# Spare wide passes on TensorE in the last head pair, the routing and the last logits; key and query chunks moved inside a pair

## The chip, the cores and the metric

## The reference

One layer over 1250 nodes of 1024 features, in three parts: a graph convolution over 20,000 edges, a kernelized attention with 16 heads of 64 and 256 random features, and a mixture of 8 experts of which each node takes two.

```python
xn = _layernorm(x)
x = x + gnn(xn, edge_index, W, b) + mix(xn[None], Wq, bq, ..., orf)[0]
x = x + ffn(_layernorm(x)[None], gate_w, gate_b, expert_w, expert_b)[0]
...
# mix: phi(y) = (exp(y @ orf.T / dk**0.25 - |y|^2 / (2 sqrt(dk))) + 1e-6) / sqrt(m)
kv = jnp.einsum('bhlm,bhld->bhmd', k_phi, v)
num = jnp.einsum('bhlm,bhmd->bhld', q_phi, kv)
out = num / einsum('bhlm,bhm->bhl', q_phi, k_phi.sum(2))[..., None]
...
# ffn: logits of 8 experts, the two largest kept, softmax over them, weighted sum of their outputs
```

## The kernel before

Products that need full precision are made of three single-pass products of a high and a low part (`xh`, `xl`; `hw[:, wi, 0]`, `hw[:, wi, 1]`). Nodes lie in 10 tiles of 128 (the last has 98 rows). The engines run side by side and are ordered by semaphores; each engine takes its instructions in the order in which the code gives them, and a wait holds all that stands behind it on that engine.

The stages are the graph's counts and products (to about 370 us), the attention (to about 964 us), the output projection in two passes of ten row tiles (to about 1093 us), the gate's logits and the routing (to about 1130 us), and the experts.

**The attention** handles two heads at a time, so there are 8 pairs. Seven run in a loop and the eighth is written out with `last=True`; its branches differ because no next pair's projections stand between its steps. In a pair TensorE runs:

- `project_third(j, wi, i, between)` (L1806 to L1808): a third of the nodes through the key, value or query weights of one pair, 24 passes of 416 or 418 columns into bank i. Behind each k but the last it can call `between(k)`, which puts another step there.
- `key_features(j, h, i)` (L1821, L1822): the random features of two tiles' keys of head h, four passes into bank 3 or 4 by turns. It waits until ScalarE has taken the exponential of the chunk two before it (`exp_done`).
- `turn_values` (L1832): values transposed into banks 6 and 7; VectorE copies them to `vt` (L1376).
- `key_values(h, ...)` (L1844): features times values into bank 5. It waits for all five key chunks of the head with their epsilon added (`kph_ready`) and for the last copied values (`aux_evac`).
- `query_features(h, i)` (L1856, L1857): two passes into bank 3 or 4 by turns; it too waits for the exponential (ScalarE, L1055) of the chunk two before it. VectorE adds the epsilon (L1363, `qph_ready`).
- `outputs(h, i)` (L1867): five tiles' attention outputs of a head; the exponentials of head 1's queries wait for both `outputs(0, ...)`, since the features of both heads share `qphi`.
- `turn(i)` (L1876): the outputs transposed; VectorE copies them to `attnT` (L1398).

In the last pair ScalarE and VectorE also make the high and low slabs of the output projection's weights (`high_slab`, `low_slab`, L1048 and L1368) between these steps. VectorE ends with two slabs, the low part of the first row tile (L1459), two copies of turned outputs and a last small low part (L1477), for which `row_tile` (L1791 to L1793) waits. GpSimd makes the weight slabs of the second pass (`split_weights`) and then the constants of the routing.

**The logits** of a tile (L1949) are eight products of 128x128 activations with 8 columns of gate weights, two passes each. `turn_x2(t)` (L1959) transposes the normalized tile before. VectorE's `choose(t)` (L1497) takes the two largest. Behind the last tile VectorE makes `both`, TensorE multiplies it (L1978, L1979: `route_done`), VectorE makes positions and one-hots (`slot_hot`), TensorE the slots (L1987) and, after three more one-hot products, the gates (L1996), between which the first gathered tile is transposed (L2008). Then the experts begin (L2022 to L2025).

Of the kernel before, what the change touches and what calls it, by code (L numbers as in the profile page):

```python
# [8 lines left out]
P = 128  # L9
N, D = 1250, 1024  # L10
TT = -(-N // P)
# [50 lines left out]
def gps_layer(nc, x, dst_pairs, src_cols, dst_cols, wg, bg, wq, bq, wk, bk, wv, bv, wo, bo, orf,  # L62
# [6 lines left out]
    with ctx:  # L69
# [217 lines left out]
        def bank(b, n=CW):  # L287
            return PB[:, 512 * b:512 * b + n]
# [356 lines left out]
        def _(pool):  # L645
# [114 lines left out]
            def split_weights(r, c):  # L760

                for k in range(KT):
                    split_slab(r, c, k)
# [23 lines left out]
            with pool.Fori(0, KT - 1) as j:  # L787
# [6 lines left out]

            attention_over(pool)
            split_weights(ro, 1)
            g.iota(iota8[:, :, :], [[0, TT], [1, E]], base=0, channel_multiplier=0,
                   allow_small_or_imprecise_dtypes=True).then_inc(s_route_const, 1)
            g.iota(thr[:, :, :], [[0, E], [P, TT]], base=P, channel_multiplier=0,
# [871 lines left out]
        def _(pe):  # L1671
# [141 lines left out]
            def key_features(j, h, i):  # L1813
# [8 lines left out]
                    ins = mm(o, nk[:, h, at], orfn[:, h], start=False, stop=True)  # L1822
                ins.then_inc(phi_done, 1)

            def pair(j, last):

                def turn_values(i):
                    t0, nt = VALUE_TILES[i]
                    pe.wait_ge(aux_evac, 12 * j + i + 1)
                    pe.wait_ge(vt_ready, 3 * j + (1, 2, 3, 3)[i])  # L1830
                    for q in range(nt):
                        ins = nc.tensor.transpose(bank(6 + i % 2)[:, q * P:(q + 1) * P],  # L1832
                                                  vT[:, (t0 + q) * P:(t0 + q + 1) * P], ident[:, :])
                    ins.then_inc(aux_done, 1)

                def key_values(h, first, last_one):

                    pe.wait_ge(kv_evac, START + 2 * j + h)
                    pe.wait_ge(kph_ready, 10 * j + 5 * h + 5)
                    pe.wait_ge(aux_evac, 2 + 12 * j + 4)  # L1840
                    for i in range(first, last_one):
                        m, t = i // TT, i % TT
                        n = LAST if t == TT - 1 else P
                        ins = mm(bank(5)[:, m * (DK + 1):(m + 1) * (DK + 1)], kphi[0:n, t, m * P:(m + 1) * P],  # L1844
                                 vt[0:n, t, h, :], start=(t == 0), stop=(t == TT - 1))
                    if last_one == MH * TT:
                        ins.then_inc(kv_done, 1)
# [23 lines left out]
                def turn(i):  # L1871

                    t0, nt = VALUE_TILES[i]
                    pe.wait_ge(aux_evac, 12 * j + 8 + i + 1)
                    for q in range(nt):
                        ins = nc.tensor.transpose(bank(6 + i % 2)[:, q * P:(q + 1) * P], att[:, t0 + q, :], ident[:, :])  # L1876
                    ins.then_inc(aux_done, 1)
# [8 lines left out]
                turn_values(2)  # L1886
                key_features(j, 1, 0)
                turn_values(3)
                key_values(0, 0, MH * TT)
                key_features(j, 1, 1)  # L1890
                project_third(j, 2, 0)
                key_features(j, 1, 2)
                key_features(j, 1, 3)
# [6 lines left out]
                query_features(0, 1)  # L1900
                if last:
                    for i in range(2, 6):
                        query_features(0, i)
                    query_features(1, 0)
                else:
                    project_third(j + 1, 0, 0, lambda k: query_features(0, 2 + k // 4) if k % 4 == 2 else None)
                    project_third(j + 1, 0, 1, lambda k: query_features(0, 4 + k // 4) if k % 4 == 2 else None)
                    query_features(1, 0)
# [3 lines left out]
                outputs(0, 1)  # L1912
                if last:
                    for i in range(2, 5):
                        query_features(1, i)
                else:
                    project_third(j + 1, 0, 2, lambda k: query_features(1, 2 + k // 2) if k % 2 == 1 else None)
                query_features(1, 5)
                pe.wait_ge(kv_evac, START + 2 * j + 2)
                outputs(1, 0)  # L1920
                outputs(1, 1)
                if not last:
                    project_third(j + 1, 1, 0)
                turn(0)
                turn(1)
                if not last:
                    key_features(j + 1, 0, 0)
                    project_third(j + 1, 1, 1)
                turn(2)
                turn(3)  # L1930

            for i in range(3):
                project_third(0, 0, i)
# [6 lines left out]
                for p in range(2):  # L1940
                    row_tile(ro, 0, 2 * g + p, p)

            def logits(t):
                if t >= 2:
                    pe.wait_ge(lg_taken, t - 1)
                for k in range(KT):
                    if k % 4 == 0:
                        pe.wait_ge(x2t_evac, 2 * t + k // 4 + 1)
                    ins = mm(bank(4 + t % 2, E), x2T[:, t % 2, k, :], gw[:, k, :], start=(k == 0), stop=(k == KT - 1))  # L1949
                ins.then_inc(lg_done, 1)  # L1950

            def turn_x2(t):
# [15 lines left out]
                    logits(t - 3)  # L1968
            logits(TT - 3)
            turn_x2(TT - 2)  # L1970
            logits(TT - 2)
            turn_x2(TT - 1)
            logits(TT - 1)

            pe.wait_ge(s_both, 1)
            whole, rest = slice(0, TT - 1), TT - 1
            for b, left in ((0, upper), (1, ones)):
                mm(bank(b, (TT - 1) * E), left[:, :], both[:, whole, :].rearrange("p t e -> p (t e)"), start=True, stop=True)  # L1978
                ins = mm(bank(b)[:, rest * E:TT * E], left[0:LAST, :], both[0:LAST, rest, :], start=True, stop=True)  # L1979
            ins.then_inc(route_done, 1)  # L1980

            for i in range(2 * TT):
                if i % TT == 0:
# [45 lines left out]
            def expert(e, par, last):  # L2030
                more, begin = tiles(pe, e)
                with pe.Fori(0, more + 1) as i:
                    tile(begin + i, e, par)

            gates(0)
            pe.wait_ge(s_cnti, 1)
            for h in range(2):
# [59 lines left out]
```

## Time and profile before

| what | value |
|---|---|
| median of 3 runs | 1418.61 us (1415.19 to 1418.94) |
| profiled execution, its own time | 1417.75 us |
| its span | 1416.2 us |
| mean granted clock of TensorE | 0.973 |
| busy: TensorE / VectorE / ScalarE / GpSimd | 96% / 56% / 40% / 26% |
| chain that ended last: TensorE / VectorE / ScalarE | 85% / 5% / 3% |

A matmul's duration in a row runs to its modelled end, and the passes overlap; how far the starts lie apart tells what one costs in a stream. A merged row (x20) runs from the first start to the last end. "Idle before" is counted from the modelled end of the instruction before.

### The profile page before, as it was taken

To read this page: it belongs to the slowest core of one execution; us is meant where nothing else is said; L and a number is where in the kernel's file an instruction comes from. 1 tells how busy PE (TensorE), PEld (TensorE's weight loads), DVE (VectorE), ACT (ScalarE), POOL (GpSimd) and SP (SyncE) were. 2 spreads that over 40 slices of the span, in tenths; PEclk is the share of its full clock that TensorE was granted. 3 is DMA by queue.
4 is the path that set the end of the run, shared out by engine and by line. 5 is a ranking of instruction groups with operands and counts; after the bars stand their busy time and mean duration, and the time that the engine had idled before them with its cause. 6 is when DMAs were issued, how large, how long until landed. Compare 5 with 4: busy or idle time off the path is not lost.

```text
span 1416.2 us, 25340 instructions
## 1 busy us (share of the span) xinstructions
PE 1354.4 (96%) x8233; PEld 1197.6 (85%) x8234; DVE 789.3 (56%) x1680; ACT 572.3 (40%) x953; POOL 364.1 (26%) x375
## 2 busy tenths in 40 slices
PE   6999999999999999999999999999999599999996
PEld 3567778999999999999999999987888588888885
DVE  7867464454466565656565656564454734444641
ACT  8543332211355454545454545451122234444440
POOL 4323333254210101010101010005023133333432
PEclk9999999999999999999999999978999599999998
DMA  5112112455200000000000000013244567777853
GB/s 185 51 49 68 42 64 68 134 158 150 64 31 16 30 15 30 15 30 15 30 15 30 15 30 0 1 60 98 72 166 148 208 183 218 220 213 211 287 134 58
DMA packets 58102, 127.78 MB, mean 90 GB/s; under 512 B 7627, under 2 KB 28827, under 8 KB 58049
## 3 DMA queue, kind: packets, MB, share of 16 engines
q1 hardware_dynamic: 48016, 96.79, 20.6%
q0 software_dynamic: 10032, 30.30, 8.7%
q8 instruction: 31, 0.51, 0.1%
q14 instruction: 23, 0.18, 0.0%
HBM read 91.46 MB, written 37.43 MB: 91 GB/s over the span
## 4 chain that ended last, share of the span: by engine, by line
PE 85%; DVE 5%; ACT 3%; issue 3%; DMA 1%; DVEq 0%; POOL 0%; POOLq 0%; SPq 0%; ACTq 0%
PE PB L1701 8%; PE PB L1806 7%; PE PB L1808 7%; PE PB L1807 7%; PE PB L2022 6%; PE PB L2023 6%; PE PB L2025 6%; PE PB L1844 5%; PE PB L1867 4%; PE PB L1751 3%; PE PB L1791 3%; PE PB L1752 3%; PE PB L1753 3%; PE PB L1792 3%; PE PB L1793 2%
## 5 line engine op out<-in xcount | busy, mean ns | idle before, releaser
L1806 PE MATMUL PB<-xh,hw 128*128 128x416 f32 (+1 forms) x576 | 203.8, 354 | 0.0
L1808 PE MATMUL PB<-xh,hw 128*128 128x416 f32 (+1 forms) x576 | 202.9, 352 | 0.0
L1807 PE MATMUL PB<-xl,hw 128*128 128x416 f32 (+1 forms) x576 | 202.8, 352 | 0.0
L2022 PE MATMUL PB<-mwh,mth 128*128 128x512 f32 x368 | 147.8, 402 | 0.3 <-issue 0.3
L2023 PE MATMUL PB<-mwl,mth 128*128 128x512 f32 x368 | 143.9, 391 | 0.0
L719 POOL CAST hw<-hraw 128x1024 fp32r<-128x1024 f32 x24 | 25.2, 1048 | 418.4 <-DVE qphi L1363 197.3
L1701 PE MATMUL PB<-ohs,ohd 128*128 128x512 bf16 x564 | 114.1, 349 | 0.3 <-DVE ohs L1226 0.3
L2025 PE MATMUL PB<-mwh,mtl 128*128 128x512 f32 x368 | 113.7, 390 | 0.0
L1807 PEld LDWEIGHTS PB<-xl,hw 128*128 128x128 f32 x576 | 108.6, 189 | 1.2
L1806 PEld LDWEIGHTS PB<-xh,hw 128*128 128x128 f32 x576 | 108.6, 189 | 1.2
L1808 PEld LDWEIGHTS PB<-xh,hw 128*128 128x128 f32 x576 | 108.5, 188 | 1.0
L1623 DVE TENSOR_TENSOR mtl<-PB,mth 128x512 fp32r<-128x512 f32 x46 | 31.8, 691 | 132.4 <-ACT mth L1141 132.4
L1226 DVE TENSOR_SCALAR ohs<-iota,sc 128x1280 bf16<-128x1280 f16 x188 | 102.8, 547 | 0.0
L1701 PEld LDWEIGHTS PB<-ohs,ohd 128*128 128x128 bf16 x564 | 45.7, 98 | 66.0 <-DVE ohs L1226 34.4
L1779 PE MATMUL PB<-hh,AT 128*128 128x256 f32 x400 | 98.2, 287 | 2.7 <-DVE hr L1252 2.7
L1780 PE MATMUL PB<-hr,AT 128*128 128x256 f32 x400 | 97.4, 285 | 0.0
L1751 PE MATMUL PB<-wqh,xh 128*128 128x256 f32 x320 | 92.1, 288 | 0.0
L1752 PE MATMUL PB<-wql,xh 128*128 128x256 f32 x320 | 90.5, 283 | 0.0
L1753 PE MATMUL PB<-wqh,xl 128*128 128x256 f32 x320 | 90.4, 283 | 0.0
L1225 DVE TENSOR_SCALAR ohd<-iota,dc 128x128 bf16<-128x128 f16 x188 | 59.8, 318 | 51.8 <-PE PB L1701 45.2
L1055 ACT ACTIVATE qphi<-PB 128x416 f32<-128x416 f32 (+1 forms) x96 | 48.3, 514 | 95.0 <-PE PB L1857 87.4
L1035 ACT ACTIVATE kphi<-PB 128x512 f32<-128x512 f32 x80 | 46.2, 598 | 96.2 <-PE PB L1844 50.6
(304 smaller groups left out, 3103.7 us busy)
## 6 DMA issues: line engine op xcount, KB each, us to landing
mraw<-expert_w SPq DMA_DIRECT2D x64, 512.0 KB, 5.8
count_rests<-ATf POOLq DMA_DIRECT2D x9, 640.0 KB, 3.3
xrow<-x SPq DMA_DIRECT2D x40, 128.0 KB, 3.0
y_scratch<-xrow SPq DMA_DIRECT2D x40, 128.0 KB, 1.9
yrow<-y_scratch SPq DMA_DIRECT2D x20, 256.0 KB, 2.9
x2n_half<-xhat SPq DMA_DIRECT2D x20, 256.0 KB, 2.4
out<-x SPq DMA_DIRECT2D x9, 512.0 KB
ATf<-wg SPq DMA_DIRECT2D x32, 128.0 KB, 2.8
```

The costliest lines, as they stand in the source:

```text
L1226: v.tensor_scalar(ohs[:, p, :], iota[:, :], sc[:, ds(col, 1)], None, ALU.is_equal).then_inc(oh_ready, 1)
L1701: ins = mm(PB[:, 1536 * s + c0:1536 * s + c0 + n], ohd[:, p, :], ohs[:, p, c0:c0 + n], start=False, stop=False, skip_group_check=True)
L1751: mm(o, xh[:, k, at], wqh[q % 2][:, k, :], start=(k == 0), stop=False)
L1752: mm(o, xh[:, k, at], wql[q % 2][:, k, :], start=False, stop=False)
L1753: ins = mm(o, xl[:, k, at], wqh[q % 2][:, k, :], start=False, stop=(k == KT - 1))
L1779: mm(o, AT[:, b, at], hh[:, q % 2, b, :], start=(b == 0), stop=False)
L1806: mm(bank(i, n), hw[:, wi, 0, k, :], xh[:, k, c0:c0 + n], start=(k == 0), stop=False)
L1807: mm(bank(i, n), hw[:, wi, 0, k, :], xl[:, k, c0:c0 + n], start=False, stop=False)
L1808: ins = mm(bank(i, n), hw[:, wi, 1, k, :], xh[:, k, c0:c0 + n], start=False, stop=(k == KT - 1))
L2022: mm(y[c], mth[:, k, :], mwh[par][:, k, c * CW:(c + 1) * CW], start=(k == 0), stop=False)
L2023: mm(y[c], mth[:, k, :], mwl[par][:, k, c * CW:(c + 1) * CW], start=False, stop=False)
L2025: ins = mm(y[c], mtl[:, k, :], mwh[par][:, k, c * CW:(c + 1) * CW], start=False, stop=(k == KT - 1))
```

## The change

It adds two helpers for TensorE. `spare(n)` issues n passes of 512 columns into bank 0 from operands that lie there, `meanwhile(n)` the same into bank 6 from the first slab of the first expert's weights. Nothing reads what they write before it is overwritten. 32 spares stand in the last pair and none in the others. Ten `meanwhile` passes stand ahead of and inside the last two tiles' logits, four behind them, 20 behind the routing product and 12 before the gates. In every pair `key_features(j, 1, 1)` stands ahead of `key_values(0, ...)`. In the seven pairs of the loop, the head 1 query chunks 2, 3 and 4 stand behind k = 2, 4 and 6 of the next pair's third projection, where they stood behind k = 1, 3 and 5. GpSimd waits for the first row tile before it writes the routing constants.

```diff
             attention_over(pool)
             split_weights(ro, 1)
+            pool.wait_ge(ro.done, 1)
             g.iota(iota8[:, :, :], [[0, TT], [1, E]], base=0, channel_multiplier=0,
...
+            def spare(n):
+
+                for _ in range(n):
+                    mm(bank(0), orfh[:, 0:P], xh[:, 0, 0:CW], start=True, stop=True)
+
             def pair(j, last):
...
                 turn_values(3)
+                key_features(j, 1, 1)
                 key_values(0, 0, MH * TT)
-                key_features(j, 1, 1)
                 project_third(j, 2, 0)
...
                 if last:
                     for i in range(2, 6):
+                        spare((0, 0, 0, 2, 5, 2)[i])
                         query_features(0, i)
                     query_features(1, 0)
...
                 outputs(0, 1)
                 if last:
                     for i in range(2, 5):
+                        spare(2)
                         query_features(1, i)
+                    spare(1)
                 else:
-                    project_third(j + 1, 0, 2, lambda k: query_features(1, 2 + k // 2) if k % 2 == 1 else None)
+                    project_third(j + 1, 0, 2, lambda k: query_features(1, 1 + k // 2) if k in (2, 4, 6) else None)
                 query_features(1, 5)
                 pe.wait_ge(kv_evac, START + 2 * j + 2)
                 outputs(1, 0)
                 outputs(1, 1)
                 if not last:
                     project_third(j + 1, 1, 0)
+                if last:
+                    spare(3)
                 turn(0)
+                if last:
+                    spare(1)
                 turn(1)
                 if not last:
                     key_features(j + 1, 0, 0)
                     project_third(j + 1, 1, 1)
+                if last:
+                    spare(2)
                 turn(2)
+                if last:
+                    spare(1)
                 turn(3)
+                if last:
+                    spare(9)
...
-            def logits(t):
+            def meanwhile(n):
+
+                for _ in range(n):
+                    mm(bank(6), mwh0[:, 0, 0:P], mwh0[:, 0, 0:CW], start=True, stop=True)
+
+            def logits(t, between=0):
...
                     ins = mm(bank(4 + t % 2, E), x2T[:, t % 2, k, :], gw[:, k, :], start=(k == 0), stop=(k == KT - 1))
+                    if between and k % 2 == 0:
+                        meanwhile(between)
                 ins.then_inc(lg_done, 1)
...
             turn_x2(TT - 2)
-            logits(TT - 2)
+            pe.wait_ge(mw_high, 1)
+            meanwhile(2)
+            logits(TT - 2, 1)
             turn_x2(TT - 1)
-            logits(TT - 1)
-
+            logits(TT - 1, 1)
+
+            meanwhile(4)
             pe.wait_ge(s_both, 1)
...
             ins.then_inc(route_done, 1)
-
+            meanwhile(20)
...
+            meanwhile(12)
             gates(0)
```

## Rows read from the trace of the kernel before

**Rows 1.** the page's slices of the span: busy tenths of TensorE, and its granted clock
```profile
PE   6999999999999999999999999999999599999996
...
PEclk9999999999999999999999999978999599999998
```

**Rows 2.** windows: us; PE, PEld, DVE, ACT, POOL busy (instructions); PEclk; DMA share; GB/s
```profile
935.00:937.50 2.50, 2.20 (x10) 1.82 (x9) 1.73 (x6) 2.06 (x5) 0.00 (x0) 0.69 0.02 7
...
970.00:972.50 2.50, 2.50 (x12) 2.08 (x11) 0.00 (x0) 0.00 (x0) 2.34 (x4) 0.99 0.39 139
```

**Rows 3.** timeline, PE, last pair: start, us, line, operation, count [idle before <- releaser]
```profile
934.71 0.42 PE L1856 MATMUL PB<-tk,orfh 128*128 128x416 f32 x1 [1.10 <-DVE nk L1347]
...
935.99 0.71 PE L1856 MATMUL PB<-tk,orfh 128*128 128x418 f32 x1 [0.30 <-ACT qphi L1055]
...
936.85 4.37 PE L1867 MATMUL PB<-kvs,qphi 128*128 128x65 f32 x20
...
964.68 0.79 PE L1791 MATMUL PB<-wh,sth 128*128 128x512 f32 x1 [2.92 <-DVE stl L1477]
```

**Rows 4.** windows, as in rows 2, at the routing
```profile
1099.00:1100.50 1.50, 1.16 (x8) 1.15 (x8) 0.05 (x1) 0.72 (x2) 0.00 (x0) 0.76 1.20 369
...
1130.50:1132.00 1.50, 1.50 (x7) 1.25 (x8) 1.43 (x5) 0.00 (x0) 0.71 (x3) 1.00 1.03 415
```

**Rows 5.** timeline, PE, the gate's logits
```profile
1094.27 3.85 PE L1949 MATMUL PB<-gw,x2T 128*128 128x8 f32 x32
...
1099.38 3.19 PE L1949 MATMUL PB<-gw,x2T 128*128 128x8 f32 x16 [0.34 <-ACT x2T L1116]
...
1104.30 3.55 PE L1949 MATMUL PB<-gw,x2T 128*128 128x8 f32 x16
```

**Rows 6.** waits of PE, 467.5 to 903.3 us: total, times, longest
```profile
PE PB L1844 <- DVE vt L1376: 3.3, 6, 0.6
PE PB L1856 <- ACT qphi L1055: 2.9, 6, 0.5
```

**Rows 7.** timeline, PE, the seventh pair
```profile
834.32 4.68 PE L1844 MATMUL PB<-vt,kphi 128*128 128x65 f32 x40 [0.56 <-DVE vt L1376]
838.81 0.36 PE L1821 MATMUL PB<-orfh,tk 128*128 128x256 f32 x1
...
839.36 0.35 PE L1806 MATMUL PB<-xh,hw 128*128 128x418 f32 x1
...
877.41 0.46 PE L1856 MATMUL PB<-tk,orfh 128*128 128x416 f32 x1 [0.49 <-ACT qphi L1055]
```

**Rows 8.** timeline, ACT, the seventh pair
```profile
832.37 0.60 ACT L1035 ACTIVATE kphi<-PB 128x512 f32<-128x512 f32 x1 [0.23 <-PE PB L1822]
...
876.87 0.89 ACT L1055 ACTIVATE qphi<-PB 128x418 f32<-128x418 f32 x2
```

**Rows 9.** timeline, DVE, the seventh pair
```profile
880.99 0.38 DVE L1363 TENSOR_SCALAR qphi<-qphi 128x416 f32<-128x416 f32 x1
```

**Rows 10.** timeline, PE, passes of the output projection at two clocks
```profile
969.96 0.45 PE L1791 MATMUL PB<-wh,sth 128*128 128x512 f32 x1
...
1082.05 0.39 PE L1792 MATMUL PB<-wl,sth 128*128 128x512 f32 x1
1082.28 0.39 PE L1793 MATMUL PB<-wh,stl 128*128 128x512 f32 x1
```

**Rows 11.** timeline, DVE, end of the last pair
```profile
960.93 1.28 DVE L1368 TENSOR_TENSOR wl<-raw,wh 128x512 fp32r<-128x512 f32 x2
```

**Rows 12.** timeline, PE, the routing and the first expert pass
```profile
1119.37 0.76 PE L1987 MATMUL PB<-hott,hotr 128*128 128x70 bf16 x10 [7.51 <-DVE hotr L1586]
...
1126.43 1.06 PE L1996 MATMUL PB<-hotg,hotr 128*128 128x105 bf16 x10 [4.88 <-DVE hotg L1618]
...
1130.39 0.53 PE L2022 MATMUL PB<-mwh,mth 128*128 128x512 f32 x1 [0.29 <-issue]
```

**Rows 13.** timeline, DVE, the last tile's choice
```profile
1107.89 0.17 DVE L1497 TENSOR_TENSOR lg<-PB,gb 128x8 f32<-128x8 f32 x1 [0.65 <-PE PB L1949]
```

## The prediction, made before the change was run

> **What bounds the kernel now.** I read the page's slices first. TensorE (PE) is busy nine tenths or more in nearly every slice, and PEclk dips twice: in the 27th and 28th slice (the last pair of heads) and in the 32nd (the routing) [rows 1]. So the time is TensorE's, and it can fall in two ways: less idle PE time in the long pair loop, or a higher granted clock in the dips. The windows show these from near. In the first the clock leaves its high level (2.4 GHz) at about 935.9 us, is at its low one (1.2 GHz) for 34 us, and is high again from 970 [rows 2]. Just before the fall PE was idle for 1.10 and 0.30 us [rows 3]. In the second it falls in the window that begins at 1099.0, and the one from 1130.5 is high again [rows 4]. Ahead of that fall lies no long idle time but a run of the gate's passes over 8 columns, 32 in 3.7 us [rows 5].
>
> Then the waits of one pair. In the six pairs from 467 to 903 us PE waited in the key products (L1844) 3.3 us in all for the copy of the values, and in the query features (L1856) 2.9 us for an exponential [rows 6]: 0.56 and 0.49 us a pair [rows 7].
>
> **The change part by part.** *Key chunk moved (8 pairs).* key_features(1, 1) goes ahead of key_values(0). Its four passes take 0.55 us where they stand, from 838.81 to 839.36 [rows 7]. In the new place PE is free from about 833.6 (the wait of 0.56 us is counted from the modelled end of the pass before) until 834.32, when the copied values are there [rows 7]. The bank it writes needs the exponential that ends at 832.97 [rows 8]: it is there. So the passes fit into the wait, and the third projection starts right behind the key products. A switch from narrow to wide passes costs about 0.08 us more: 0.47 us a pair gained. ScalarE's next exponential waits for the key products, which start as before; nothing comes later.
>
> *Query chunks moved (7 pairs).* The three query chunks inside the projection stand one step of k later, so three more passes of 0.19 us lie ahead of the one that waits until 877.41 for the exponential begun at 876.87 [rows 7, 8]. The wait shrinks to under 0.1 us, and one step fewer remains behind it: 0.56 us gained. What could be late next is outputs(1, 0), which wants VectorE's fourth eps pass; this ends at 881.37 [rows 9], and PE would arrive at about 881.9. Bounds of either move: nothing, if the neighbour engine only moves the wait, and 0.56. I take 7 x 1.03 + 0.47 = **7.7 us**.
>
> *Spares in the last pair.* 32 passes of 128x512, each into a bank that nobody reads. No row shows such a pass itself; the nearest are the output projection's, of the same width: 0.23 us apart at the high level [rows 10], and at the low one twelve between 964.68 and 969.96, 0.44 [rows 3, 10]. Nine stand in the idle time before the old fall: 2.1 us of work for 1.4 us of waits [rows 3] and 0.3 of a third; the last two delay one query chunk by 0.46, which the 0.30 us wait behind it nearly pays. With no hole left there I expect the clock to stay high. The chain is then, from 936.0: a query chunk 0.46; outputs(0, 0), 20 passes, which took 4.37 us at the low level [rows 3] and should take 2.2, as 40 of the same form take 4.49 in the key products [rows 7]; another chunk and outputs(0, 1), to 941.3. Here the next exponential starts only after outputs(0, 1), so PE waits until 942.1 with two spares inside; four query chunks and five spares to 944.8; outputs(1, 0) and (1, 1) to 949.2; three spares 0.7; the turns, paced by VectorE's copies, to 951.7. Now VectorE is last: from its two slabs (960.93 now) to the first pass of the output projection (964.68) lie 3.75 us [rows 3, 11], none of them TensorE's. So the projection begins at about 955.5 instead of 964.68: **9.1 us**, rounded down. The last nine spares (2.1 us) lie beside these 3.75; without this cover they would cost 2.1. The first passes of the projection, twelve at 0.44, take 0.23 each: **2.5 us**. Bounds of the two terms: all of 11.6, or the fourth rival.
>
> *The wait on GpSimd* stands behind split_weights, which keeps GpSimd busy from 970 on [rows 2], with sixteen steps of which four fit into 2.5 us; the first row tile is done long before its end. Behind it are queued the routing constants, wanted at 1109. Zero on both sides.
>
> *Spares in the logits and the routing.* The last two tiles' logits get four each, two stand ahead, four behind; 20 come after the first routing product, 12 before the gates. But the 3.7 us run of 8-column passes gets none, and it is what stands ahead of the old fall [rows 4, 5]. I take it that the clock falls there again. Then the spares cost 0.43: the two ahead 0.85 less 0.34 that PE waited anyway, and four in each tile's logits 1.7 (3.4 to 5.1, nearest row 3.55) [rows 5]; together **+3.9 us** before the last logits are out, and VectorE's routing chain begins with them. The four behind lie in the wait for `both`. The 20 fill the 7.51 us wait for the one-hots [rows 12]: as a dense stream at the low level they resemble 964.68 to 970, where the clock came back after 5.3 us. 5.3 at 0.43 are 12 passes, the other 8 take 1.8, sum 7.1: just covered (8.6 and 1.1 too long if it stays low). Then the gates and the first transposes find the high level. From 1126.43 to 1130.39 they took 3.96 us [rows 12]; half of PE's part goes, ScalarE's and VectorE's steps stay: **-1.2 us**.
>
> A rule speaks on this last part. The trace: the clock was high from 1130.5 on, right behind 20 gate passes and 8 transposes [rows 4, 12]. The Trainium skill ("TensorE: Matmul & The Clock Gate", Part 4: PE-mode transpose) says that the full clock doesn't engage for transposes, which don't count as work in the same way. By that rule this rise should have come later; the trace disagrees.
>
> **Sum**, against the profiled execution's 1417.75 us (span 1416.2): 1417.75 - 7.7 - 9.1 - 2.5 + 3.9 - 1.2 = **1401.2 us**. That execution is 0.9 us under the median of the three runs; the forecast stays at 1401.
>
> **The rivals.** (1) *The clock holds through the logits.* The spares ahead of and inside the last two catch it in time. Then I estimate the last logits start by ScalarE's slab at 1104.1 instead of 1104.30 and run 2.6 us instead of 3.55, and VectorE, busy with three slabs until about 1107.0, makes its last choice 0.9 us earlier than at 1107.89 [rows 5, 13]; the routing products halve, 0.9; the gates gain between 0 and 1.2 (PE idles for 3 us behind its 20 spares), say 0.8. 1417.75 - 19.3 - 2.6 = 1395.9. For it: logits with a spare behind every second product are much denser. Against: the bare run is untouched. Chance 0.30; the forecast 0.46.
> (2) *The clock falls late in the last pair*, among the turns or in the last VectorE chain, where PE still idles some 1.5 us behind its nine spares. Then the projection begins slow for 5.3 us as now, 2.5 us come back, and a turn or two are slower: 1401.2 + 2.5 to 3.5, about 1404. The skill's rule on transposes (same page and section) would favour this. Against: seven spares stand among the turns and nine behind. Chance 0.12.
> (3) *The moves in the pair do nothing*: the waits come back at the next chunk, ScalarE and VectorE setting the pace. 1401.2 + 7.7 = 1408.9. Against: what the moved chunks need is there in time [rows 8, 9]. Chance 0.08.
> (4) *Slower: the spares pay at the low clock.* If it still falls at 936, 25 spares at 0.43, 10.7 us, stand on PE's path against about 4.2 us of waits (0.30 and 2.92 among them [rows 3]), +6.5; the logits +3.9, and 0.2 from 20 slow spares: 1417.75 - 7.7 + 6.5 + 3.9 + 0.2 = 1420.7. It decides from where the nine early spares don't keep the clock up. Against: the hole they fill is the only one there. Chance 0.04.
>
> **How the numbers follow.** About 0.3% (4.3 us) is what a measurement of this kernel can tell from no change. The forecast and rivals (1) to (3) lie more than that below 1418.6; (4) lies within it, or beyond with some further loss. Faster 0.94, same 0.04, slower 0.02. The range goes from 1393.5, the first rival with the upper bounds of its terms, to 1408, short of (3).
>
> **What would show it.** The waits of L1844 and L1856 in a pair are under 0.2 us, and the pairs follow each other about 1.0 us closer. The granted clock is 1.00 from 900 to the second dip, and the output projection starts 9 us closer to the last pair's key products. In the logits, spares 0.43 us apart and 5.1 us a tile (forecast), or 0.22 and 2.6 (first rival). The clock is high at the gates. The prediction is wrong if the clock drops in the last pair all the same, or holds where I let it fall.

## The result and the profile after

| | before | changed |
|---|---|---|
| median, 8 executions each | 1418.3 us (1412.2 to 1424.6) | 1402.8 us (1397.2 to 1414.1) |
| profiled execution, its own time | 1417.75 us | 1404.21 us |
| its span / mean granted clock | 1416.2 us / 0.973 | 1402.7 us / 0.988 |

The ratio changed to before is 0.9905, 95% interval 0.9879 to 0.9930: faster by about 1%. A second measurement (e9 below) gave 0.9929 (0.9908 to 0.9951).

The page's slices of the changed kernel (busy tenths of TensorE and its granted clock), which answer to [rows 1]:

```profile
PE   6999999999999999999999999999999899999996
...
PEclk9999999999999999999999999999999799999998
```

The dip at the last pair is gone, the one at the routing is shallower (7 for 5). Windows of the changed kernel, from the last pair on (columns as in rows 2):

```profile
901.70:930.00 28.30, 28.30 (x184) 27.41 (x185) 16.63 (x37) 16.48 (x31) 0.00 (x0) 1.00 0.12 38
930.00:949.60 19.60, 18.57 (x128) 16.50 (x126) 13.61 (x32) 9.61 (x19) 0.00 (x0) 1.00 0.17 55
949.60:970.00 20.40, 20.34 (x90) 16.82 (x91) 9.94 (x11) 3.75 (x4) 14.61 (x14) 1.00 0.57 168
```

and at the logits and the routing:

```profile
1076.00:1081.00 5.00, 4.96 (x46) 4.87 (x45) 4.30 (x15) 1.09 (x2) 1.27 (x2) 1.00 0.34 107
1081.00:1094.50 13.50, 13.50 (x55) 12.24 (x54) 4.72 (x11) 8.28 (x10) 0.00 (x0) 0.50 1.00 365
1094.50:1101.40 6.90, 6.67 (x20) 5.18 (x21) 4.74 (x25) 0.21 (x1) 0.00 (x0) 0.50 0.08 30
1101.40:1108.30 6.90, 4.49 (x37) 3.42 (x36) 6.56 (x17) 0.00 (x0) 0.00 (x0) 0.99 0.00 0
1108.30:1111.70 3.40, 3.40 (x10) 2.62 (x9) 3.06 (x14) 0.00 (x0) 1.81 (x2) 0.50 0.07 18
1111.70:1118.00 6.30, 3.83 (x35) 2.88 (x34) 4.01 (x8) 1.19 (x2) 2.59 (x5) 1.00 0.56 173
```

PEclk is 1.00 through the whole last pair. It falls at the logits all the same, comes back inside the 20 spares (from 1101.4), falls once more from 1108.3 to 1111.7 and is high at the gates.

In the pairs, the waits of PE from 467.5 to 901 us, against [rows 6]:

```profile
PE PB L1838 <- DVE vt L1377: 1.6, 6, 0.3
```

The key products (L1850 now) and the query features (L1862 now) are gone from the list; only the value transposes' 0.27 us is left. The end of the last pair, TensorE's timeline, against [rows 3]:

```profile
927.93 1.33 PE L1829 MATMUL PB<-xh,orfh 128*128 128x512 f32 x5
929.09 0.39 PE L1862 MATMUL PB<-tk,orfh 128*128 128x416 f32 x1
...
930.84 2.34 PE L1873 MATMUL PB<-kvs,qphi 128*128 128x65 f32 x20
...
946.31 2.35 PE L1829 MATMUL PB<-xh,orfh 128*128 128x512 f32 x9
949.66 0.50 PE L1792 MATMUL PB<-wh,sth 128*128 128x512 f32 x1 [1.00 <-DVE stl L1478]
```

The five spares (L1829) stand where PE waited 1.10 us, and the chunk behind them follows without a wait. An `outputs` of 20 passes takes 2.34 us instead of 4.37. The nine last spares end 1.00 us ahead of the output projection (2.92 us of waiting before).

For the whole document it helps to cut a trace into stages by the start of a fixed instruction. These distances come from the traces' rows, one profiled execution each:

| stage, us | before | changed | forecast of the difference | measured |
|---|---|---|---|---|
| seven pairs, first to eighth key products (L1844) | 507.97 | 501.17 | -7.2 | -6.8 |
| eighth key products to first output projection | 57.88 | 48.00 | -9.6 | -9.9 |
| output projection to the bare logits (tile 6) | 129.59 | 127.09 | -2.5 | -2.5 |
| bare logits to the last logits pass | 13.22 | 17.57 | +3.9 | +4.35 |
| last logits pass to the slots' first pass (L1987) | 11.88 | 11.89 | 0 | 0.0 |
| slots' first pass to the gates (L1996) | 7.05 | 7.05 | 0 | 0.0 |
| gates to the first expert pass (L2022) | 3.97 | 3.99 | -1.2 | 0.0 |
| first expert pass to the end | 285.8 | 285.4 | 0 | -0.4 |

The changed kernel's profiled execution reaches the first key products 1.7 us late (400.50 for 398.83). Up to there the programs differ only by one key chunk that stands in a wait, and its second trace (e9) reaches them at 399.01, so this is not the change's. With the gates' 1.2 that didn't come and the 0.45 more at the logits it makes up the 3 us by which the execution lies over the forecast of 1401.2.

### The profile page after: what moved, and what is told of

Read it like the earlier page. It is cut to its first block, busy times and chain, and to the rows that moved or that the text cites. A ratio compares the mean times of both kernels' runs of the same rounds, so it can differ in the third digit from the quotient of the medians.

```text
span 1402.7 us, 25462 instructions
## 1 busy us (share of the span) xinstructions
PE 1359.7 (97%) x8277; PEld 1203.1 (86%) x8312; DVE 789.8 (56%) x1680; ACT 571.5 (41%) x953; POOL 362.0 (26%) x375
## 4 chain that ended last, share of the span: by engine, by line
PE 88%; DVE 5%; issue 2%; ACT 2%; DMA 2%; DVEq 0%; POOL 0%; POOLq 0%; SPq 0%; ACTq 0%
PE PB L1702 8%; PE PB L1807 7%; PE PB L1809 7%; PE PB L1808 7%; PE PB L2051 6%; PE PB L2052 6%; PE PB L2054 6%; PE PB L1850 5%; PE PB L1873 5%; PE PB L1752 3%; PE PB L1792 3%; PE PB L1794 3%; PE PB L1753 3%; PE PB L1754 3%; PE PB L1793 3%
## 5 line engine op out<-in xcount | busy, mean ns | idle before, releaser
L1702 PE MATMUL PB<-ohs,ohd 128*128 128x512 bf16 (+1 forms) x530 | 110.3, 348 | 3.4 <-DVE ohs L1227 0.7
L1142 ACT ACTIVATE mth<-PB 128x512 fp32r<-128x512 f32 x46 | 27.5, 598 | 139.1 <-PE PB L2037 139.1
```

The source lines that it names most:

```text
L1702: ins = mm(PB[:, 1536 * s + c0:1536 * s + c0 + n], ohd[:, p, :], ohs[:, p, c0:c0 + n], start=False, stop=False, skip_group_check=True)
```

## The experiments

**How executions of one kernel differ.** The executions of before spread over 22 us (48 of them, 1407.8 to 1430.4). Each comes with its span and mean granted clock, so the time that it spent at the low level is 2 x (1 - clock) x span: 51 us in the fastest, 100 to 103 in the slowest two. I fitted one straight line through 130 executions of ten kernels, with one slope for all and a level for each. The slope is 0.39 us of time for a microsecond at the low clock (95% interval 0.36 to 0.42), and what is left over has a standard deviation of 1.7 us. Without the slowest execution of before neither the slope nor any level moves by more than 0.1. The level tells what an edit costs or gains at equal clock, and the mean low-clock time what it does to the clock:

| kernel | executions | mean us | low clock, mean us | level against before |
|---|---|---|---|---|
| before | 48 | 1417.7 | 69 | 0 |
| changed (with e9) | 14 | 1404.0 | 35 | -0.2 +- 1.5 |
| e1: moves only | 7 | 1406.5 | 61 | -7.9 +- 1.4 |
| e2: last pair's spares only | 12 | 1412.9 | 53 | +1.7 +- 1.2 |
| e3: logits' and routing's spares only | 12 | 1417.0 | 50 | +6.9 +- 1.3 |
| e5: moves and last pair's spares | 6 | 1402.4 | 47 | -6.7 +- 1.6 |
| e4 and e10: changed without 14 logit spares | 11 | 1401.2 | 35 | -3.3 +- 1.6 |
| e11: e4 without the last nine | 6 | 1402.0 | 36 | -2.8 +- 1.8 |
| e6: spares in two more logits | 6 | 1404.4 | 33 | +0.7 +- 1.9 |
| e7: changed without the early nine | 8 | 1407.2 | 45 | -1.0 +- 1.5 |

The slope is a mean over stages, and the +- are 95% intervals. Low-clock time in a stage where TensorE waits anyway costs less than 0.39 (e5 below shows such a stage), and an edit that removes only such time shows a level that is too high; this matters for e3, and in part for every kernel with spares at the routing.

**e1, the moves alone.**

```diff
-                key_values(0, 0, MH * TT)
                 key_features(j, 1, 1)
+                key_values(0, 0, MH * TT)
...
-                    project_third(j + 1, 0, 2, lambda k: query_features(1, 2 + k // 2) if k % 2 == 1 else None)
+                    project_third(j + 1, 0, 2, lambda k: query_features(1, 1 + k // 2) if k in (2, 4, 6) else None)
```

> The kernel before with the key and query chunks moved and no spare pass. My theory: the moves alone are worth 7.7 us by the rows; a pair's period falls from about 72.6 to about 71.6 us, whatever the clock does elsewhere, so the ratio to before is about 0.9945 (7.7 of 1418). Rival (the waits only move to the next chunk): period unchanged, ratio 1.000. A second rival: the moves thin out other stretches so that the clock falls in the loop in some executions; then single executions come out above before's slowest and the mean granted clock is lower than before's.

Measured: median 1405.1, ratio 0.9908 (0.9875 to 0.9940), more than the 0.9945 expected. The chain of its profile puts the key products every 71.6 us (470.58, 542.22, 613.85; in before 471.29, 543.74):

```profile
470.58 4.68 PE PB L1844 x40
...
542.22 4.68 PE PB L1844 x40
...
613.85 4.68 PE PB L1844 x40
```

At equal clock the level is -7.9, the forecast's 7.7. The rest of the mean's 11.2 us goes with 9 us less at the low clock, but the seven executions lie between 48 and 79 us of it and before's between 51 and 103; whether the fuller loop keeps the clock up better, or seven executions fell well, stays open. The rival "the waits only move on" is out. The second rival (clock falls in the loop) didn't show: the slowest of the seven took 1412.2 us, and the trace's loop ran at the high level.

**e8 and e12, each move alone**, the halves of e1's diff.

> The kernel before with the key chunk moved alone. By the forecast's terms the distance of one pair's key products from the next's falls by 0.47 us, from 72.6 to 72.1, and no L1844 waits over 0.2 us; the wait of the query chunk (0.49 us) stays. Rival (the wait only moves on): distance 72.6, a new wait in front of the third projection or of the next key chunk.

> The kernel before with the query chunks moved alone. By the forecast's term the distance between the pairs' key products falls by 0.56 us, from 72.6 to 72.05, and the wait of L1856 for the exponential is under 0.1 us. Measured with the key move alone: 0.43 us, and both together 0.95 to 1.0; so 0.50 to 0.56 is left for this one. Rival (the exponential is what sets the pace, and the wait only moves to the next query chunk): distance unchanged.

Measured, as distances between key products, in one execution each (1415.6 and 1412.8 us as a whole). Key move: from the second pair (470.79) to the seventh (831.71) five distances of 72.2 us, before 72.6: 0.4 us. Query move: 474.50 to 906.42, six distances of 71.99: 0.6 us. The waits of PE in the pairs, key move first:

```profile
PE PB L1856 <- ACT qphi L1055: 2.9, 6, 0.5
PE PB L1832 <- DVE vt L1376: 1.6, 6, 0.3
```

```profile
PE PB L1844 <- DVE vt L1376: 3.3, 6, 0.6
PE PB L1832 <- DVE vt L1376: 1.6, 6, 0.3
```

Each move takes away its own wait and leaves the other's as it was in [rows 6]. The two are of the size foreseen (0.47 and 0.56), and together they make what e1 has (0.95 us a pair).

The trace of e12 shows one thing more. It has no spare, and PE waits 0.96 us and 0.29 us in the last pair where before it waited 1.10 and 0.30. Its clock fell there too, at 934.4, but for 3.4 us and not for 34, and once more for 6.8 us from 954.9. Three rows of its chain:

```profile
906.42 4.65 PE PB L1844 x40
...
934.28 0.57 PE PB L1856
...
955.74 0.80 PE PB L1791
```

From the key products to the output projection it took 49.3 us, 8.6 less than before's 57.9, and 0.8 more than the 48.5 with 32 spares (e2 below). So the long dip that the spares remove is not there in every execution.

**e2, the last pair's spares alone.** The 32 `spare` passes and GpSimd's wait; no moves, nothing in the logits or behind.

> The kernel before with only the 32 spares of the last pair (and GpSimd's wait). My theory: the clock stays at its high level from the last pair to the logits in every execution, and the output projection starts 9.1 us closer to the last pair's key products than in the profile of before (964.68 - 906.79 = 57.9 us there, so about 48.8 here), and the first row tile gains 2.5 us more: 11.6 us, ratio 0.992. Rival (the clock falls late in the turns): about 8 to 9 us, with PEclk 0.50 behind the turns. Rival (in most executions of before the clock holds in the last pair anyway and the profiled one was an unlucky one): the two kernels' times overlap, and the ratio is over 0.996.

Measured: median 1414.4, ratio 0.9957 (0.9930 to 0.9984). In its profile the eighth key products to the output projection is 48.49 us (9.4 less than before's) and on to the bare logits 127.10 (2.5 less): in that execution all of the 11.9 us is there. In the mean it is 4.8 us, because the mean execution of before is not the profiled one: it has 69 us at the low clock, the profiled one 76, and 33 of the 48 have 71 or less. So the second rival (the profiled one was an unlucky one) is partly right: the times overlap, though the ratio is just under 0.996. The stages bear out the mechanism where the dip is there, and the forecast took one execution's dip for every one's.

**e3, the routing's spares alone.** Ten ahead of and inside the last logits, 4, 20 and 12 behind; no moves, none in the last pair.

> The kernel before with only the spares of the logits and the routing (10 ahead of and inside the logits, 4, 20 and 12). My theory, as the profile of the changed kernel showed it: where the clock falls in the bare logits before them, the spares cost 0.43 each and the last logits come 3.9 us later; the gates gain nothing, since the gather's landing follows: about +4 us, ratio 1.003. Where the clock holds, about -2.6 us, ratio 0.998. Rival (the spares hold the clock in most executions): ratio under 0.999.

Measured: ratio 0.9988 (0.9960 to 1.0017), no difference. In its profiled execution the clock held through the bare run of 32 narrow passes and the first of the two tiles with spares, and fell at 1112.5, inside the second, behind a wait of 2.00 us:

```profile
1100.29 3.85 PE L1959 MATMUL PB<-gw,x2T 128*128 128x8 f32 x32
...
1111.17 0.36 PE L1959 MATMUL PB<-gw,x2T 128*128 128x8 f32 x2 [2.00 <-ACT x2T L1116]
```

Bare logits to the last pass took 14.58 us, where the changed kernel has 17.57 and before 13.22. So with the clock up TensorE waits for ScalarE, and the stage is still no shorter than with a low clock and no spares. Its mean low-clock time is 20 us under before's, worth 7.6 us by the slope, and its mean is 0.7 us better. So the 20 us that were won seem to have lain mostly where TensorE waits, and its level of +6.9 can't be read as a price of passes. The fall in the bare logits, as in the changed kernel's trace, would take away only some 7 us; so the rival, that the spares hold the clock in most executions, may well be right, but one trace and a ratio with 1 in its interval don't decide it.

**e4 and e10, without the 14 logit spares.**

```diff
-            pe.wait_ge(mw_high, 1)
-            meanwhile(2)
-            logits(TT - 2, 1)
+            logits(TT - 2)
             turn_x2(TT - 1)
-            logits(TT - 1, 1)
-            meanwhile(4)
+            logits(TT - 1)
+            pe.wait_ge(mw_high, 1)
```

> The changed kernel without the spares ahead of, inside and directly behind the last two tiles' logits (14 passes); the 20 and the 12 of the routing stay. My theory: these 14 are what costs; the last logits come 3.9 us earlier than in the changed kernel's profile, the clock still rises in the 20. So about 4 us faster than the changed kernel: ratio to before about 0.988 where the changed kernel has 0.9905. Rival (without them the 20 do not lift the clock, or the logits' spares pay in the executions where the clock holds): no faster than the changed kernel, ratio 0.9905 or more.

> The changed kernel without the 14 logit spares, a second time. My theory: the 14 cost 2 to 4 us, so it is again 2 to 4 us faster than the changed kernel on this chip (about 1400 to 1401), with the same time at the low clock within 5 us. Rival (the first measurement's 2 us were chance, and the 14 are free): within 1 us of the changed kernel.

Measured: 0.9872 (0.9841 to 0.9904), and the second time 0.9893 (0.9878 to 0.9908), beside 0.9929 for the changed kernel on the same chip. The stage from the bare logits to the last pass is 14.56 and 13.90 us, 3.0 and 3.7 less than the changed kernel's 17.57 and 17.61. Low-clock time is the same, 35 us. This is the fastest kernel of the study, 2.8 us under the changed one in the mean of 11 and 14 executions; the intervals of the ratios overlap or touch, but the stage that was edited shows the difference in both pairs of traces. How much it is depends on where in the logits the clock falls: without logit spares the stage took 13.1 to 15.2 us over nine traces, with them 17.0 to 17.6 in the three traces in which the clock fell in the bare run.

**e5, no spare behind the last pair.** e4 without the 20 and the 12 too.

> The changed kernel without any spare in the logits and the routing (48 passes left out); moves and the last pair's spares stay. A line through the executions of each kernel (time against time at the low clock, which follows from the mean granted clock and the span) has so far given two prices: moves 8.2 us less at equal clock, last pair's spares 1.2 more, routing's spares 6.3 more, and 0.38 us for each us at the low clock. My theory (the parts add up): 8.2 + 5.8 = 14 us under before in the mean, about 1404.7, ratio 0.990; that is, the 48 routing spares give back nothing in sum. Rival (the 20 spares behind the routing product pay, since they lift the clock for what follows): slower than the kernel without the 14 logit spares by 4 us or more, ratio 0.990 against its 0.987. These differ only by that kernel: if this one comes out at 0.987 or less, the 20 and 12 are worth nothing.

Measured: 0.9899 (0.9878 to 0.9919), mean 1402.4: between e4 and the changed kernel. Both sides had named a ratio of 0.990, so it doesn't tell them apart; the distance to e4 and e10 does, 1.2 us in the mean. Its clock stays low for 34 us at the routing, and costs nothing that the stages can show: slots to gates 7.05 us, gates to experts 3.95 us, as with the 32 spares (7.05, 3.99). Its windows at the routing:

```profile
1094.00:1108.40 14.40, 1.53 (x20) 1.20 (x20) 13.41 (x40) 0.00 (x0) 2.57 (x2) 0.50 0.07 21
1108.40:1112.40 4.00, 3.67 (x28) 3.38 (x28) 1.18 (x3) 1.19 (x2) 0.99 (x2) 0.50 0.47 154
1112.40:1118.00 5.60, 5.57 (x20) 4.57 (x21) 4.30 (x7) 1.16 (x1) 2.49 (x4) 0.81 0.96 355
```

TensorE is busy 1.5 of 14.4 us while VectorE is busy 13.4: nothing here waits for TensorE. What is left for the 32 is the first experts' passes, where e5's clock is still low for part of the window from 1112.4 (0.81). That is 2.1 us of 5.6 at the low level, at half speed about 1 us of work. The "4 us or more" of the rival is not there.

**e6, spares in the logits of tiles 6 and 7 too.**

```diff
-                    logits(t - 3)
-            logits(TT - 3)
+                    if t == TT - 1:
+                        pe.wait_ge(mw_high, 1)
+                    logits(t - 3, int(t == TT - 1))
+            logits(TT - 3, 1)
```

> The changed kernel with spares inside the logits of tiles 6 and 7 too (8 more passes, so that the bare run of 32 narrow passes ahead of the old fall is gone). My theory: what brings the clock down at the logits is that bare run; with it filled, the clock holds until the routing, time at the low clock falls by about 20 us a run, worth 7 to 8, less 1.7 us for the 8 passes at the high clock: about 1397, ratio 0.985. Rival (the narrow passes are not what brings it down, or the passes cost more than they hold): clock still falls between the logits of tile 6 and 9, ratio 0.990 or more.

Measured: 0.9916 (0.9894 to 0.9938), not the 0.985 I gave. In its profile the clock stays up through all four logits and falls at 1091.8, after PE has idled for 1.33 us behind them.

```profile
1076.00:1084.00 8.00, 8.00 (x61) 7.34 (x60) 3.72 (x17) 1.84 (x4) 1.28 (x2) 1.00 0.71 237
1084.00:1091.00 7.00, 5.96 (x41) 4.96 (x40) 5.22 (x15) 5.79 (x7) 0.00 (x0) 1.00 1.01 356
1091.00:1098.00 7.00, 6.18 (x19) 5.22 (x20) 5.07 (x24) 1.16 (x2) 0.00 (x0) 0.56 0.45 183
```

Bare-logits-to-last-pass is 13.67 us. That is 3.9 us better than the changed kernel, and still 0.4 worse than before's 13.22 with a low clock and no spares. What held the clock cost as much as the clock gave. The sum I had made was wrong in its first term, twice. The 20 us less at the low clock weren't there: from the logits to the gates this profile has 13.7 us of it where the changed kernel's has 23.9, and the mean over executions is 33 us where the changed kernel has 35. And I priced that time at the slope of the whole kernel, in a stage where it costs less. The executions are no faster than the changed kernel's (mean 1404.4).

**e7, without the early nine.**

```diff
-                        spare((0, 0, 0, 2, 5, 2)[i])
+                        spare((0, 0, 0, 0, 0, 0)[i])
```

> The changed kernel without the nine spares ahead of head 0's query chunks in the last pair; the other 23 stay. My theory: the nine fill the only hole in front of the old fall; without them the clock falls there in many executions as in before (a stretch of 34 us at the low clock in its profile), and then later spares run at 0.43: 4 to 9 us slower than the changed kernel in the mean, ratio 0.994 to 0.996. Rival (the hole is too thin to matter in most executions, and it was the spares behind it that kept the clock): within 1.5 us of the changed kernel.

Measured: median 1408.4, ratio 0.9931 (0.9904 to 0.9958), mean 3.2 us over the changed kernel, 10 us more at the low clock. That is a little under the 4 to 9 us expected, and the ratio's interval overlaps the changed kernel's; the trace has to carry the argument. Its profiled execution falls at the old place; windows, and two rows of TensorE's timeline from the low stretch:

```profile
926.00:930.00 4.00, 2.98 (x14) 2.65 (x14) 2.72 (x8) 2.92 (x7) 0.00 (x0) 0.79 0.02 4
930.00:940.00 10.00, 10.00 (x42) 9.47 (x43) 3.88 (x9) 1.80 (x5) 0.00 (x0) 0.50 0.17 52
940.00:943.00 3.00, 3.00 (x13) 2.63 (x11) 1.13 (x4) 1.21 (x3) 0.00 (x0) 0.67 0.56 175
943.00:953.00 10.00, 9.37 (x67) 8.18 (x65) 7.31 (x15) 3.86 (x9) 0.00 (x0) 1.00 0.01 2
```

```profile
928.60 4.37 PE L1873 MATMUL PB<-kvs,qphi 128*128 128x65 f32 x20
...
939.40 1.06 PE L1829 MATMUL PB<-xh,orfh 128*128 128x512 f32 x2
```

The stage to the output projection is 54.05 us there, 6.05 over the changed kernel's. The clock came back at about 942, behind six of the seven spares among head 1's query chunks, where in before it stayed low until 970. Whether those spares brought it back isn't shown: in e12 it came back at 937.8 with no spare at all. Two of the eight executions were faster than the changed kernel's median (1400.6, 1401.0, with 25 and 36 us at the low clock): without the nine the fall is likely, not certain.

**e9, the changed kernel again.**

> The changed kernel itself once more, on the same chip as the next two, so that these can be compared with it directly. Expected: ratio 0.990 to 0.991 as in its first measurement, mean time at the low clock about 32 us.

Measured: median 1404.1, ratio 0.9929 (0.9908 to 0.9951), 28 to 51 us at the low clock, 38 in the mean: a little less gain than the 0.990 to 0.991 expected, with 6 us more at the low clock. Its stages are those of the first trace to 0.1 us: 47.95, 127.11, 17.61, 11.90, 7.05, 4.10.

**e11, e10 without the last nine.** `spare(9)` behind the last turn is left out.

> The kernel of e10 without the nine spares behind the last turn. My theory: they lie beside VectorE's last chain of 3.75 us and cost nothing, and they guard the clock over it; without them the chain is a hole of 3.5 us and the clock falls there in many executions, which makes the first row tile slow: 1 to 5 us slower than e10 in the mean, 5 to 10 us more time at the low clock. Rival (seven spares among the turns are enough): within 1 us of e10.

Measured: 0.9901 (0.9878 to 0.9923), mean 0.5 us over e10 and 1 us more at the low clock. In its profiled execution the clock did fall there, once, at 950 for 3.4 us, and the stage from the output projection on is 128.69 us, 1.6 over the others. The cover is as forecast (the output projection starts 47.99 us after the key products with or without the nine), and so is the mechanism, but not the frequency. By the mean the rival is right: 0.5 us lies within its 1 us.

## Why the prediction was right, point by point

- **Moves, 7.7 us.** Measured -6.8 in the seven pairs and -0.5 in the eighth (57.34 in e1 for 57.88), 7.3 us; e1's level is -7.9. Each wait went with its own move.
- **Last pair, 9.1 and 2.5 us.** Measured 9.4 (48.00, less the key move's 0.5) and 2.5. VectorE's chain was what stood last: 3.74 us from its two slabs (945.92) to the projection, before 3.75. PE's wait in front of the projection is 1.00 us. The 9.4 is measured against an execution with the long dip; against e12 with its short one it is 0.8.
- **The clock falls again at the logits, +3.9 us.** Measured +4.35. The bare run is there unchanged, the clock falls behind it and the spares stand apart by the low clock's price. Timeline of the changed kernel, against [rows 5]:

```profile
1076.76 3.84 PE L1973 MATMUL PB<-gw,x2T 128*128 128x8 f32 x32
...
1083.43 0.85 PE L1973 MATMUL PB<-gw,x2T 128*128 128x8 f32 x4
1084.14 0.77 PE L1965 MATMUL PB<-mwh 128*128 128x512 f32 x1
1084.71 0.85 PE L1973 MATMUL PB<-gw,x2T 128*128 128x8 f32 x4
...
1098.55 6.16 PE L1965 MATMUL PB<-mwh 128*128 128x512 f32 x20
```

  From one spare to the next 1.28 us, of which four narrow passes are 0.85 and a wide one 0.43. That it is the bare run which brings the clock down is likely, not shown. In twelve of the thirteen traces in which the run stands bare the clock fell 2.4 to 5.6 us after its start; in e6, which filled it, the clock held. But in e3, where it stood bare too, the clock also held, for 12.2 us. The size has some luck in it as well: before's 13.22 us is among the shortest of the nine traces without logit spares, 13.1 to 15.2. The 20 took 6.16 us (7.1 forecast), as the clock came back 2.9 us into them and not 5.3, and ended ahead of the one-hots.
- **Gates, -1.2 us: this term failed.** Measured 0.0, though the clock was high. TensorE's own part did shrink, but what follows is not TensorE's:

```profile
1113.28 0.66 PE L2025 MATMUL PB<-hotg,hotr 128*128 128x105 bf16 x10 [0.73 <-DVE hotg L1619]
1113.78 0.61 PE L2037 MATMUL PB<-ident,xg 128*128 128x128 f32 x4
1114.81 0.66 PE L2037 MATMUL PB<-ident,xg 128*128 128x128 f32 x4 [0.42 <-DMA xg<-x2n_half,slots]
1115.30 0.65 PE L2025 MATMUL PB<-hotg,hotr 128*128 128x105 bf16 x10
1117.27 0.49 PE L2051 MATMUL PB<-mwh,mth 128*128 128x512 f32 x1 [1.31 <-DVE mtl L1624]
```

  0.42 us are lost on the second gather, 1.31 us in front of the first expert pass. The profile gives VectorE's `mtl` for the latter, but the half that this pass needs was made at 1115.9 and the other at 1116.8. The weight load of the same pass says otherwise:

```profile
1117.26 0.19 PEld L2051 LDWEIGHTS PB<-mwh,mth 128*128 128x128 f32 x1 [1.47 <-issue]
```

  It names issue, time in which the engine waited for nothing that the profile shows. TensorE's sequencer loads the expert's tile counts from memory here:

```profile
L424 PEldq TENSOR_LOAD <-cnti x8: 300/308/1074, 1115.1 to 1350.9; - x8
```

  The first of these loads starts at 1115.1, 2.2 us ahead of the pass; two of them, 0.31 us each, stand there with their checks and branches. In before the first load stands just as far ahead of the pass (1128.2 for 1130.39). That this chain is what keeps the stage at 4 us is read from the traces alone. With that, gates to experts is 3.95 to 4.10 us in thirteen of the fourteen traces, at either clock; in the fourteenth, e11, the second gather's wait is 0.54 us and the stage 4.25. The forecast let ScalarE's and VectorE's steps stay and counted neither on the gather nor on the sequencer. No run tried to shorten either.
- **What it got right by luck.** The sum was made from one execution. Executions of before differ by 22 us, as the clock falls or holds at several places. The profiled one has 76 us at the low clock, more than 37 of the 48 have, and with it the long dip in the last pair on which 11.6 us of the sum rest; e12 shows the same place with a short one. Yet its time lies 0.9 us under the median of the first three, so the sum landed near the median too. Other executions fall at other places: e10, for instance, fell in the first pair, at 398.6, after a wait of 1.8 us for `vt`, and stayed low to 412.2. Windows of e10 there:

```profile
395.00:398.60 3.60, 1.76 (x15) 1.55 (x13) 3.60 (x7) 0.71 (x2) 1.29 (x1) 1.00 0.34 112
398.60:412.20 13.60, 13.59 (x56) 13.10 (x55) 1.38 (x4) 1.09 (x2) 3.38 (x2) 0.50 0.15 49
412.20:420.00 7.80, 7.80 (x46) 7.68 (x45) 2.81 (x7) 4.90 (x9) 0.00 (x0) 1.00 0.00 0
```

  The seven pairs then take 506.8 us instead of 501.2. The same instructions, with the same wait, kept the clock in [rows 2]'s kernel and in the changed one. So by the fit the mean gain of the change, 13.7 us of 1417.7, is nearly all in the 35 us less at the low clock (13.5 at 0.39 a microsecond), and at equal clock the moves' 7.9 and the spares' own passes cancel. That split is only as good as one slope for all stages: where the low-clock time was won while TensorE waited, it gave less than 0.39, and the passes cost less than the level says.
- **The rivals.** (1) did not come in the profiled executions of the changed kernel; in its fastest (1397.2, mean clock 0.994, some 17 us at the low level in all) the clock must have held nearly everywhere behind the start, but no trace of such a one was taken. (2) is out in both traces of the changed kernel and was seen once without the last nine (e11). (3) is refuted by e1, e8 and e12. (4) is refuted by the windows, and its point of decision, the early nine, is borne out by e7's trace.
- **The wait on GpSimd** has no run of its own. The stages that use its constants take the same time with and without it (last logits to slots 11.88 and 11.89 us, slots to gates 7.05 and 7.05), as forecast.
- **The range.** Its lower end, 1393.5, doesn't come out of the bounds that it names: with 0.56 us for each of the 15 moves and 1.2 at the gates the first rival gives 1394.7. Nothing hangs on it.
- The rule of the Trainium skill on transposes that the prediction weighed ("TensorE: Matmul & The Clock Gate", Part 4: PE-mode transpose): the rise at 1130.5 speaks against it less clearly than was said, since of PE's work right ahead of it about half was the 20 gate passes, 2.1 us beside 1.9 of transposes. In the changed kernel the ten turns, with seven spares among them, stand in a stretch at 1.00. That trace can't tell whether the spares were needed for it; e11 left out only those behind.

## What to carry to other kernels

Fill a wait with work that has to be done anyway before filling it with spare passes: the two moves gave about 7 us whatever the clock did, while the last pair's spares gave 9.4 us beside an execution in which it had fallen for long and 0.8 beside one in which it had fallen briefly. Price low-clock time by the stage: where TensorE is the bound it cost 9.4 of 29 us in the last pair, where VectorE is the bound it cost nothing that the stages show, and a spare pass among narrow ones is pure cost once the clock has fallen. And take the spread of a kernel's executions with their granted clocks before making a sum on one of them.

## What had not been expected of the hardware

- Two programs equal up to a point, with the same waits at that point, differ from execution to execution in whether the clock falls there: the wait of 1.8 to 1.9 us in the first pair was followed by a fall in three of fourteen traces (e3, e10, e12; 10 to 14 us each) and not in the others. The eleven others all have a fall of 3.4 us at about 315, which these three lack.
- In e10 the clock was low through all 40 key products over 65 columns, 8.8 us in which TensorE was never idle, and came back at 412.2, 4.8 us into the wide passes of a projection. Narrow work doesn't always stand before a low clock, though: in e12 it came back at 937.8 among the 20 narrow passes of an `outputs`, and in before behind the gates and the first transposes [rows 4].
- The time of an execution follows its time at the low clock closely, 0.39 us per us with 1.7 us left over.
